# Side steps handed out tile by tile, the opening reordered, and two waits left out on TensorE

## What is computed

```python
h = layernorm(x);  q = h Wq' + bq;  k = ctx Wk' + bk;  v = ctx Wv' + bv
p = softmax(where(mask <= 0.5, clip(q k' / 4, -50, 50), -10000))
d = rs * ((p v) Wo' + bo);  x = x + tanh(g0) * (layernorm(d) * gamma + beta)
y = layernorm(x);  top2, idx = top_k(y Wrouter, 2);  w = softmax(top2)
out = x + tanh(g1) * sum_e w[e] * square(relu(y Wfc[e])) Wproj[e]
```

## Time and profile before

| | us |
|---|---|
| median of 3 runs | 1176.19 (1175.33 to 1176.25) |
| the profiled execution, its own time | 1174.79 |
| its span, first to last instruction | 1172.5 |
| TensorE busy | 1122.5 (96% of the span) |
| VectorE busy | 861.9 (74%) |
| ScalarE busy | 663.9 (57%) |
| GpSimd busy | 156.2 (13%) |

### The profile page before, as it was taken

How to read it: one execution, slowest core, us unless ns; L and a number is a source line. 1 busy time by engine, 2 the same in 40 slices (tenths; PEclk the granted TensorE clock), 3 DMA queues, 4 the chain that set the end, 5 groups by cost and what they waited for, 6 DMA issues and landing times.

```text
span 1172.5 us, 55936 instructions
## 1 busy us (share of the span) xinstructions
PE 1122.5 (96%) x24824; PEld 1075.5 (92%) x24824; DVE 861.9 (74%) x2004; ACT 663.9 (57%) x846; POOL 156.2 (13%) x186
## 2 busy tenths in 40 slices
PE   6899999999999999999999999999999999999784
PEld 5899999999999999999999999999999999988784
DVE  5567677777777777777777777777777777777667
ACT  3556565656565665656565656656565655554332
POOL 0000000011010111010111101010101100124421
PEclk9899999999999999999999999999999999999988
DMA  4212221212122222212121222212222212134306
GB/s 155 63 51 70 68 69 40 81 62 76 50 77 69 75 60 71 69 48 80 61 77 48 77 70 76 70 60 69 65 63 61 74 50 75 49 105 115 92 26 168
DMA packets 44654, 84.63 MB, mean 72 GB/s; under 512 B 12866, under 2 KB 27202, under 8 KB 44418
## 3 DMA queue, kind: packets, MB, share of 16 engines
q1 hardware_dynamic: 34706, 65.62, 19.2%
q10 hardware_dynamic: 6832, 8.92, 2.3%
q0 software_dynamic: 2880, 6.53, 1.5%
HBM read 70.32 MB, written 10.79 MB: 69 GB/s over the span
## 4 chain that ended last, share of the span: by engine, by line
PE 82%; DVE 13%; issue 2%; DMA 1%; ACT 1%; POOL 0%; SPq 0%; DVEq 0%; ACTq 0%; POOLq 0%
PE v_ps L615 22%; PE k_ps L618 21%; PE sc_ps L641 18%; PE o_ps L656 11%; DVE prob L1292 3%; DVE vst L1089 2%; DVE kl L1074 2%; PE sc_ps L558 1%; PE k_ps L673 1%; PE k_ps L680 1%; PE sc_ps L559 1%; PE sc_ps L560 1%; DVE c_lo L1080 1%; DMA raw<-in_ctxT 1%; DVE q_hi L1126 1%
## 5 line engine op out<-in xcount | busy, mean ns | idle before, releaser
L911 ACT ACTIVATE prob<-sc_ps,m_bias 125x896 f32<-125x896 f32 x384 | 377.4, 1009 | 327.7 <-PE sc_ps L641 327.3
L615 PE MATMUL v_ps<-wv_hi,c_hi 64*125 64x256 f32 x1520 | 311.5, 285 | 3.4 <-DVE c_lo L1080 2.8
L618 PE MATMUL k_ps<-c_hi,wk_hi 64*128 64x500 f32 x760 | 306.3, 403 | 0.0
L615 PE MATMUL v_ps<-wv_hi,c_lo 64*125 64x256 f32 x1520 | 301.5, 278 | 0.0
L615 PE MATMUL v_ps<-wv_lo,c_hi 64*125 64x256 f32 x1520 | 301.5, 278 | 0.0
L618 PE MATMUL k_ps<-c_lo,wk_hi 64*128 64x500 f32 x760 | 293.6, 386 | 0.0
L618 PE MATMUL k_ps<-c_hi,wk_lo 64*128 64x500 f32 x760 | 292.8, 385 | 0.0
L1089 DVE TENSOR_TENSOR vst<-v_ps,rowv 125x512 f32<-125x512 f32 x191 | 131.4, 688 | 181.2 <-PE v_ps L615 181.2
L1292 DVE TENSOR_SCALAR prob<-prob 125x896 f32<-125x896 f32 x384 | 235.6, 626 | 20.0 <-ACT prob L911 20.0
L615 PEld LDWEIGHTS v_ps<-wv_hi,c_hi 64*125 64x125 f32 x1520 | 226.6, 184 | 17.7 <-issue 6.3
L615 PEld LDWEIGHTS v_ps<-wv_hi,c_lo 64*125 64x125 f32 x1520 | 229.9, 183 | 0.0
(11 more groups left out here) (194 smaller groups left out, 1662.9 us busy)
## 6 DMA issues: line engine op xcount, KB each, us to landing
raw<-in_ctxT SPq DMA_DIRECT2D x96, 500.0 KB, 3.5
rows<-slot_rows SPq DMA_DIRECT2D x32, 132.0 KB, 2.2
w_raw<-in_we ACTq DMA_DIRECT2D x16, 256.0 KB, 4.8
rec<-inv_scratch SPq DMA_DIRECT2D x64, 56.0 KB, 2.0
expert_out<-expert_rows SPq DMA_DIRECT2D x6, 448.0 KB, 7.9
xq<-in_x ACTq DMA_DIRECT2D x16, 112.0 KB, 3.8
xr<-in_x ACTq DMA_DIRECT2D x16, 112.0 KB, 3.5
out_y<-acc SPq DMA_DIRECT2D x3, 448.0 KB, 3.1
```

The costliest lines, as they stand in the source:

```text
L615: v_last = pe.matmul(v_ps[0:TC, j * D:(j + 1) * D], c_s[v_rows, cs], w_m[v_rows, k, :], start=begin and j == 0, stop=end, skip_group_check ...
L618: k_last = pe.matmul(k_ps[:, half, 0:TG], w[k_rows, k, ws], c_m[k_rows, :], start=begin, stop=end)
L911: act.activation(prob[0:TC, c % PB, :].rearrange("p (c n) -> p c n", c=2), sc_ps[0:TC, 2 * (c % 2):2 * (c % 2) + 2, 0:NH * S // 2], ACT.Ex ...
```

## The change

1. *Side steps.* `step` goes. A table `BESIDE` gives each side step its loop step. What stood together at one step is split over several: `x_after` becomes `x_centre`, `x_gamma`, `x_new`; the top two of the last two pairs are found for both at once (8 columns x 2), in five pieces; their weights in three. The weights of the 14 sent pairs, made apart before (`route_difference(0)` in the last pair, `route_weights(0)` at step 6), are now made together with those of the last two. Of the steps on TensorE `out_proj` goes from step 12 to 10, `y_transpose` from 18 to 20; the router stays at 23. GpSimd's two reciprocal roots follow the sends 10 and 15 instead of 11 and 13.
2. *Waits on TensorE.* In the tiles `fc(u)` no longer waits for `yslo_done` (the wait of `turn(u + 2)` just ahead asks for a higher count) and `proj(u)` no longer for `hlo_done` (the wait of `hidden_turn` just ahead asks for the same count). They stay where there is no such wait ahead.
3. *Opening.* TensorE makes the first keys ahead of the first queries. VectorE makes `m_bias` and `kl` ahead of the queries' steps, and the low part of context group 1 ahead of `q_high` and `q_low`. The first `kv_part` asks for one `v_evac` instead of two. ScalarE rounds the weights ahead of the copy `xnT`, and takes `kh` ahead of the second `c_hi`. SyncE issues context group 1 ahead of the mask.
4. *Steps 32 to 39.* VectorE does `take(u - 2)` ahead of `hidden_low(u)`, and no longer waits for its own sums to raise `y2_evac`; TensorE waits for `acc_done` directly.

```diff
+BESIDE = {"sums": 3, "divide": 6, "out_proj": 10, "delta": 11, "delta_stat": 12, "centre": 14, "gamma": 15, "x_new": 16,
+          "x_stat": 17, "y_rows": 19, "y_turn": 20, "y_low": 22, "router": 23, "logits": 24, "most": 25, "first": 26,
+          "next": 27, "next_first": 28, "second": 29, "exps": 30, "sum": 31, "share": 32, "w_tok": 33}
...
-        def step(at):
-            return {0: 0, 2: 3, 4: 6, 7: 12, 8: 14, 9: 15, 11: 18, 12: 20, 14: 23, 15: 24, 17: 26, 18: 28}[at]
...
             sp.dma_start(wv[:, :, :], a["wv"]).then_inc(wv_in, 16)
+            sp.dma_start(raw[:, 1, :, :], a["ctxT"][1]).then_inc(raw_in[1], 16)
             sp.dma_start(mask_i[0:TC, :], a["mask"]).then_inc(mask_in, 16)
-            sp.dma_start(raw[:, 1, :, :], a["ctxT"][1]).then_inc(raw_in[1], 16)
...
-                if u == 11:
+                if u == BESIDE["delta"] - 1:
                     x_plus_beta(NP - 1)
                     inv_std(1, NP - 1)
-                if u == 13:
+                if u == BESIDE["x_stat"] - 2:
                     inv_std(2, NP - 1)
...
-                    wait(pe, v_evac, 2 * n + half)
+                    wait(pe, v_evac, 1 if n == 1 and half == 0 else 2 * n + half)
...
-            pe.wait_ge(wq_in, 16)
-            q_proj(0, first_side)
             pe.wait_ge(wlo_done, 1)
             k_proj(0, 0, 0)
             k_proj(0, 1, 0)
+            pe.wait_ge(wq_in, 16)
+            q_proj(0, first_side)
...
                 wait(pe, relu_done, u - 1)
                 if u < NU:
-                    pe.wait_ge(yslo_done, u + 1)
+                    if u + 2 >= NU:
+                        pe.wait_ge(yslo_done, u + 1)
...
-                pe.wait_ge(hlo_done, u + 1)
-                wait(pe, y2_evac, u - 1)
+                if u >= NU - 1:
+                    pe.wait_ge(hlo_done, u + 1)
+                wait(pe, y2_evac, min(u - 1, NU))
+                wait(pe, acc_done, 2 * (u - 1 - NU))
...
-                if u == step(7):
+                if u == BESIDE["out_proj"]:
                     pe.wait_ge(ylo_done, NP)
                     out_proj(NP - 1)
-                if u == step(11):
+                if u == BESIDE["y_turn"]:
                     y_transpose(NP - 1)
-                if u == step(14):
+                if u == BESIDE["router"]:
...
-            x_transposed(0, first_side)
             for src, dst, arrived in ((wk, wk_hi, wk_in), (wv, wv_hi, wv_in)):
                 act.wait_ge(arrived, 16)
                 act.activation(dst[:, :, :], src[:, :, :], ACT.Copy).then_inc(whi_done, 1)
+            x_transposed(0, first_side)
+            act.wait_ge(cst_in, 16)
+            for m in range(KD):
+                k_hi_evac(0, m, 0)
...
+            def x_centre(i):
                 normalised(1, i, dlt, dlt).then_inc(x1_step, 1)
+            def x_gamma(i):
                 dve.wait_ge(x1_step, 2 * i + 1)
                 dve.tensor_tensor(dlt[0:PW, :], dlt[0:PW, :], gam[0:PW, :], ALU.mult).then_inc(x1_step, 1)
+            def x_new(i):
...
+            ctx_low(0, 0, 0)
             normalised(0, 0, xn, xq).then_inc(xn_done, 1)
-            ctx_low(0, 0, 0)
             ctx_low(0, 1, 0)
             for i, (src, hi, lo) in enumerate(((wk, wk_hi, wk_lo), (wv, wv_hi, wv_lo))):
                 dve.wait_ge(whi_done, i + 1)
                 dve.tensor_tensor(lo[:, :, :], src[:, :, :], plain(hi[:, :, :]), ALU.subtract).then_inc(wlo_done, 1)
             dve.wait_ge(cst_in, 16)
+            dve.wait_ge(mask_in, 16)
+            dve.tensor_scalar(m_bias[0:TC, :], mask_i[0:TC, :], 0.5, -FAR, ALU.is_le, ALU.mult).then_inc(m_ready, 1)
+            for m in range(KD):
+                k_lo_evac(0, m, 0)
             q_evac(0, first_side)
             q_split(0, 0)
+            for k in range(KD):
+                ctx_low(1, k, 1)
+            dve.wait_ge(row_in, 16)
+            dve.wait_ge(ones_done, 2)
+            v_evac_step(0, 0, 0)
             q_high(0, 0)
             q_low(0, 0)
-            dve.wait_ge(mask_in, 16)
-            dve.tensor_scalar(m_bias[0:TC, :], mask_i[0:TC, :], 0.5, -FAR, ALU.is_le, ALU.mult).then_inc(m_ready, 1)
-            dve.wait_ge(row_in, 16)
-            dve.wait_ge(ones_done, 2)
-            for m in range(KD):
-                k_lo_evac(0, m, 0)
-            for half in range(2):
-                v_evac_step(0, half, 0)
+            v_evac_step(0, 1, 0)
...
-                dve.wait_ge(acc_done, 2 * e + 2)
-                dve.sem_inc(y2_evac, 1)
...
-                if at == 7:
-                    delta(NP - 1)
-                    delta_statistics(NP - 1)
-                if at == 8:
-                    x_after(NP - 1)
-                    x_after_statistics(NP - 1)
-                if at == 9:
-                    y_rows(NP - 1)
...
+                if u == BESIDE["delta"]:
+                    delta(last)
+                if u == BESIDE["delta_stat"]:
+                    delta_statistics(last)
+                if u == BESIDE["centre"]:
+                    x_centre(last)
+                if u == BESIDE["gamma"]:
+                    x_gamma(last)
+                if u == BESIDE["x_new"]:
+                    x_new(last)
+                if u == BESIDE["x_stat"]:
+                    x_after_statistics(last)
+                if u == BESIDE["y_rows"]:
+                    y_rows(last)
...
+                if u >= 2:
+                    take(u - 2)
                 if u >= NU:
                     hidden_low(u)
-                if u >= 2:
-                    take(u - 2)
-                for at in (0, 2, 4, 7, 8, 9, 12, 15, 18):
-                    if step(at) == u:
-                        beside_experts(at)
+                beside_experts(u)
```

135 lines of the change are left out of this document (79 added, 56 removed).

## The result

| | before | after |
|---|---|---|
| median, us | 1175.88 (1175.33 to 1176.25, 4 runs) | 1154.89 (1153.46 to 1155.07, 4 runs) |
| the profiled execution, its own time | 1174.79 | 1154.87 |
| its span | 1172.5 | 1152.9 |

The ratio is 0.9819 (95% interval 0.9802 to 0.9836): 21.0 us less, where I had forecast 16.7. Of the 21.0 us the two traces show 19.6. Of the other 1.4, 1.1 are the distance of the profiled execution of before from its median (1174.79 to 1175.88), which I had carried over as constant and which the changed kernel doesn't have (1154.87 to 1154.89); 0.3 are the time around the span, 2.3 us before and 2.0 after.

The account below looks back on a forecast made before the run. TensorE, busy in 96% of the span, was taken as the bound, held up by waits for VectorE. 12.6 - 1.3 + 1.9 + 1.6 + 1.9 = 16.7 us less gave a median of 1159.5 us, range 1156.0 to 1164.0.

Parts of the forecast that it names:

- Two waits of TensorE: In the tiles, fc's dropped wait saves 0.07 us a tile, proj's nothing: 1.9 us gained, bounds 0 and 3.8.
- both removed waits pay: Rival: TensorE's sequencer is late through the whole tile, so the gain is 3.8 us: 1157.6 us; chance 0.12.
- Packing: Before out_proj, moved to step 10: a new wait for the packing DMAs, -1.3 us, bounds -0.4 and -2.4.
- Lumps: Steps 2 to 32: TensorE's waits for VectorE's lumped side steps go, with the lower clock: 12.6 us, bounds 9.5 and 13.
- Opening: Before the tiles: VectorE's new order, with the mask at 13.5, brings TensorE's work forward: 1.6 us, bounds 0.5 and 2.8.
- Steps 32 to 39: Last steps: sums fill VectorE's wait for ScalarE, so TensorE stays the bound: 1.9 us, bounds 1.2 and 2.3.
- The last additions: After the last proj: sums over the loaded outputs and the output DMAs, taken as unchanged.
- The median: Whole kernel: the median stays 1.4 us above the profiled execution, giving 1159.5 us against 1158.1.

Follow-up runs that it names:

- s_side_alone: The kernel before with only the new side-step table; both waits in, old opening, old steps 32 to 39: 1172.41 us, ratio 0.9911.
- d_p4: The changed kernel with four long-met waits (hlo_done, relu_done, sq_done, hhi_done) added at proj(u) beside y2_evac: ratio 0.9870.
- x_best: The changed kernel without sq_done at hidden_turn, turn's wait for rows moved to proj, out_proj and what follows one step later: ratio 0.9825.
- the changed kernel's second run: The changed kernel measured again, nothing altered, on a chip with longer attention: 1163.18 us, ratio 0.9830.
- first and third: Runs of the unaltered changed kernel: first 1154.89 us, ratio 0.9819; third, on a chip with longer attention, 1162.51 us, ratio 0.9828.

## Why the forecast was wrong, point by point

- *Two waits of TensorE: the step that failed.* Forecast 1.9 us with the ends 0 and 3.8; the runs give 4.3 to 4.9 (65.2 of s_side_alone less 60.4 to 60.95; 4.3 to 4.5 on its own kind of chip). I priced `fc`'s wait by one pair of starts, 0.07 us; over the tiles it is 0.09. I set `proj`'s to nothing because the timeline has no idle time in front of `proj`. It costs 1.6 us, and its cost comes out at the next `turn`, 0.26 us behind the last matmul with this wait and 0.17 without (medians). The rival "both removed waits pay" was the right mechanism, but with twice 0.07 too cheap. The rule of the Trainium skill that I had cited (Advanced Engine Details and Errata, Network/Comms: 50 to 100 ns for reading a semaphore from a sequencer on TRN2) would have given 2.8 to 5.6 us for both, an estimate, and the measured 4.3 to 4.9 lie within. By the runs only waits with an instruction of their own cost that: the only wait of a place, taken away, changed 0.2 to 0.3 us over all tiles.
- *What I could have read.* The trace of before has a row for TensorE's list at `fc`'s wait and one for the load from `tab`, and in the timeline of the weight loads a row for each plain `turn`:

```profile
L833 PEldq EVENT_SEMAPHORE  x30: 51/51/51, 1055.0 to 1130.0; - x30
```

```profile
L824 PEldq TENSOR_LOAD <-tab x32: 297/302/492, 1051.0 to 1129.4; - x32
```

```profile
1074.70 0.20 PEld L706 LDWEIGHTS v_ps<-cst,rows 128*128 128x128 f32 x2 [0.16 <-issue]
```

  The first says that this wait is an instruction of 51 ns, the second, by my reading above, that the list is hardly ever held back in a plain tile. The third says that the weight loads stand idle for 0.16 us with nothing to wait for. Over the tiles the median of that is 0.17 us before, 0.05 in the changed kernel, 0.25 in d_p4 and 0.03 in x_best. I asked what TensorE's matmuls wait for and not what its list does.
- *Packing: forecast -1.3, result 0 in the first trace.* The sign and the place were right in s_side_alone (-1.0) and in ten others (waits of 0.09 to 0.89 us, 0.36 in the changed kernel's second run), but in its first and third there is none. In the first the packing began 1.9 us sooner behind the start of the fourth send than before, which nothing in the trace of before shows.
- *Lumps: 12.6 forecast, 11.8 shown, up to 12.3 if the kind of chip counts for 0.5.* All fit into the tile as worked out; no wait for `ys_lo` above 0.3 us is left, and the clock stays at its upper level (1.00). What I had at nothing is the 0.9 us that `share` and `w_tok` cost in steps 32 and 33 under the old order there.
- *Opening: 1.6 forecast, 1.43 in the first pair of traces, 2.7 to 2.8 by all.* That the first pair agrees is luck, and so in part are its starts, 17.69 and 23.78 for 18.0 and 24.3. The mask was there at 12.34, before even my lower bound of 12.7, and 1.2 us before the 13.5 that I took. But from there to the first `kv_part` it took 5.35 us and not 4.5: VectorE stood idle for 0.81 us between the two `kl`, waiting for ScalarE's `kh`, which my chain didn't have.
- *Steps 32 to 39: 1.9 forecast, 2.05 in the first traces,* with the order of VectorE and the period of 2.74 us as described. That sum hides 2.95 from the new order and 0.9 lost by the new table. The last additions took 0.54 of it back, which I had called unchanged.
- *The median.* I carried the 1.4 us between profiled execution and median over, and the 2.3 around the span; together the changed kernel has 1.4 less of them. The time lies 1.1 us below the range, so without this, or without the 3.0 us of the waits, or without the 1.3 of the packing, it would have been inside.
